# Second layer before the correction in PSUM, and score maxima subtracted by four full-array products

## The reference

```python
pos = grid_q[:, :, None, :] - grid_kv[:, None, :, :]
bias = jnp.sign(pos) * jnp.log1p(jnp.abs(pos))
bias = jax.nn.relu(bias @ cpb_w1 + cpb_b1)      # 2 -> 32
bias = jax.nn.relu(bias @ cpb_w2 + cpb_b2)      # 32 -> 32
bias = (bias @ cpb_w3 + cpb_b3)                 # 32 -> 1
sim = jnp.einsum('bhid,bhjd->bhij', qh, kh) + bias
attn = jax.nn.softmax(sim, axis=-1)
```

## Time and profile before

| | us |
|---|---|
| median of 3 runs | 929.76 (927.41 to 930.8) |
| the profiled execution | 930.51 |
| its span | 928.7 |
| TensorE matmuls busy | 848.8 (91%) |
| VectorE busy | 713.9 (77%) |
| ScalarE busy | 639.5 (69%) |
| GpSimd busy | 59.9 (6%) |
| granted TensorE clock, mean | 0.970 |

### The profile page before, as it was taken

One profiled execution on the slowest core, in us unless ns is written; L12 is line 12 of the kernel. 1 busy time (PEld: TensorE's weight loads), 2 busy tenths in 40 slices (PEclk: granted clock), 3 DMA queues, 4 the chain that ended last, 5 costly groups with the idle time before them and its releaser, 6 DMA issues.

```text
span 928.7 us, 34427 instructions
## 1 busy us (share of the span) xinstructions
PE 848.8 (91%) x15908; PEld 300.5 (32%) x15908; DVE 713.9 (77%) x472; ACT 639.5 (69%) x717; POOL 59.9 (6%) x40
## 2 busy tenths in 40 slices
PE   2179999989999999989999999999999999999936
PEld 1123323333333333323333333323333333333312
DVE  3678799898878659998878849989887749888411
ACT  1347768867777858877776857896777757777711
POOL 2200002120000002040000002040000000000000
PEclk9589999999999999999999999999999999999978
DMA  4210101011101101002011101002011101000010
GB/s 146 59 52 3 50 2 50 7 49 13 51 10 41 28 2 49 8 14 48 26 28 27 50 1 50 9 2 57 5 51 27 50 1 43 11 3 3 2 48 23
DMA packets 29535, 27.89 MB, mean 30 GB/s; under 512 B 22096, under 2 KB 24016, under 8 KB 29392
## 3 DMA queue, kind: packets, MB, share of 16 engines
q1 hardware_dynamic: 29392, 25.69, 10.6%
HBM read 23.05 MB, written 2.49 MB: 27 GB/s over the span
## 4 chain that ended last, share of the span: by engine, by line
PE 83%; DVE 8%; ACT 3%; DMA 3%; issue 2%; SPq 0%; POOL 0%; ACTq 0%; POOLq 0%; DVEq 0%
PE pair L771 29%; PE scores L783 24%; PE pair L766 9%; PE scores L795 3%; PE pair L914 3%; PE scores L880 3%; DVE h L565 3%; PE pair L924 3%; PE pair L873 2%; ACT h L426 2%; DVE big L668 2%; PE pair L891 1%; PE pair L905 1%; PE pair L818 1%; PE pair L854 1%
## 5 line engine op out<-in xcount | busy, mean ns | idle before, releaser
L426 ACT ACTIVATE h<-pair 128x1024 f32<-128x1024 f32 x512 | 496.5, 1022 | 201.9 <-PE pair L771 201.6
L565 DVE TENSOR_TENSOR h<-hx,hy 128x2048 f32<-128x2048 f32 x256 | 579.9, 2300 | 41.4 <-PE pair L771 41.1
L771 PE MATMUL pair<-h,wts 32*32 32x512 f32 x8192 | 346.6, 597 | 9.7 <-DVE h L565 9.7
L783 PE MATMUL scores<-h,wts 128*32 128x512 f32 x2048 | 273.6, 606 | 0.9 <-ACT h L426 0.9
L771 PEld LDWEIGHTS pair<-h,wts 32*32 32x32 f32 x8192 | 135.2, 103 | 29.3 <-DVE h L565 13.5
L766 PE MATMUL pair<-fy,u_rows 32*32 32x512 bf16 x4096 | 118.7, 386 | 27.4 <-DMA fy<-fy_dram 20.1
L783 PEld LDWEIGHTS scores<-h,wts 128*32 128x32 f32 x2048 | 43.6, 108 | 209.2 <-issue 208.4
L766 PEld LDWEIGHTS pair<-fy,u_rows 32*32 32x32 bf16 x4096 | 37.6, 88 | 196.7 <-issue 178.4
L691 DVE TENSOR_REDUCE neg_max<-pair 128x8 f32<-128x512 f32 x32 | 22.1, 691 | 70.3 <-PE pair L873 70.3
L306 POOL TENSOR_TENSOR conv_prod<-qpad,wts 128x288 f32<-128x288 f32 x16 | 21.6, 1379 | 440.3 <-ACT qpad L452 440.3
L406 POOL TENSOR_TENSOR big<-big,hat_x 128x512 f32<-128x512 f32 x16 | 35.5, 2248 | 119.0 <-DVE big L662 119.0
(11 more groups left out here) (87 smaller groups left out, 342.6 us busy)
## 6 DMA issues: line engine op xcount, KB each, us to landing
hx<-features_dram SPq DMA_DIRECT2D x64, 128.0 KB, 2.7
hy<-features_dram SPq DMA_DIRECT2D x64, 128.0 KB, 3.1
att_den<-reciprocals_dram SPq DMA_DIRECT2D x4, 512.0 KB
wts<-weights_dram SPq DMA_DIRECT2D x2, 960.0 KB, 8.5
fy_dram<-fy_part SPq DMA_DIRECT2D x96, 8.0 KB, 1.5
x<-x_dram SPq DMA_DIRECT2D x2, 512.0 KB, 5.9
fy<-fy_dram SPq DMA_DIRECT2D x64, 12.0 KB
out_dram<-x SPq DMA_DIRECT2D x2, 512.0 KB, 4.9
```

What stands on the lines that cost most here:

```text
L426: emptied("z", 2 * g + j, act.activation(h2[g % H2_BUFS][:, 2 * j:2 * (j + 1)].rearrange("p r n -> p (r n)"), pair_of("z", 2 * g + j)[:], ...
L565: dve.tensor_tensor(h1[g % H1_BUFS][:].rearrange("p c (y x) -> p c y x", x=W), hx[unit % 2][:, :, t].unsqueeze(2).broadcast_to([128, CT, H ...
L771: ins = pe.matmul(z[r][32 * c:32 * (c + 1)], w(l, "w2")[key[r], key[r]], h1[g % H1_BUFS][key[r], c], start=False, stop=True)
L783: ins = pe.matmul(scores[phase % 2][32 * r:32 * (r + 1)], w(l, "w3")[:, 32 * t:32 * (t + 1)], h2[g % H2_BUFS][:, r], start=False, stop=t = ...
```

## The change

Two edits and shifts of slots. (1) In `layer2` the 16 second-layer products come first, with `start=True` and the waits for the pairs, behind the wait for `h1_ready`; the 16 corrections follow with `start=False` and hand the pairs over, and the waits for `fy` and `u_rows` stand between them. (2) GpSimd copies `neg_max` to `neg_max_wide` (128 x 8 x 64, fp32r) in a new stage `widen_max`, which waits for the maxima and for the previous `max_off`; `score_max` waits for the copy of two phases before and not for `max_off`; `max_off` waits for the copy and takes four products of 128x128 in fp32r with an fp32r copy of the identity, which VectorE makes in its set-up. (3) `max_off` and `exp` move from step 2 to step 3 of the next phase; `exp_sums` from 3 to 4 and `attend` from 4 to 5; GpSimd's first hat products from 42 to 44, `sample` from 47 to 49, its copy to 51, keys and values to 52.

```diff
--- before.py
+++ after.py
@@ -80,20 +80,21 @@
     ("act", "features", 0): 36, ("act", "spread_out", 0): 37, ("dve", "features_sign", 0): 39,
     ("act", "distances", 0): 38, ("act", "distances", 1): 39, ("act", "distances", 2): 40,
     ("act", "distances", 3): 41, ("dve", "hats", 0): 42, ("dve", "hats", 1): 44,
-    ("pool", "hat_products", 0): 42, ("pool", "hat_products", 1): 44, ("dve", "hat_products", 0): 45,
-    ("dve", "hat_products", 1): 46, ("pe", "sample", 0): 47, ("dve", "sample_out", 0): 49,
-    ("pe", "keys_values", 0): 50, ("act", "keys_values_out", 0): 50,
+    ("pool", "hat_products", 0): 44, ("pool", "hat_products", 1): 44, ("dve", "hat_products", 0): 45,
+    ("dve", "hat_products", 1): 46, ("pe", "sample", 0): 49, ("dve", "sample_out", 0): 51,
+    ("pe", "keys_values", 0): 52, ("act", "keys_values_out", 0): 52,
 }
 
 AFTER_SLOTS = {
-    ("pe", "exp_sums", 0): 3, ("act", "exp_sums_out", 0): 3, ("pe", "attend", 0): 4,
-    ("act", "attend_out", 0): 4, ("dve", "reciprocal", 0): 8, ("dve", "divide", 0): 12, ("pe", "project", 0): 12,
+    ("pe", "exp_sums", 0): 4, ("act", "exp_sums_out", 0): 4, ("pe", "attend", 0): 5,
+    ("act", "attend_out", 0): 5, ("dve", "reciprocal", 0): 8, ("dve", "divide", 0): 12, ("pe", "project", 0): 12,
     ("dve", "residual1", 0): 14, ("pe", "mlp_up", 0): 14, ("act", "mlp_gelu", 0): 14, ("pe", "mlp_up", 1): 15,
     ("act", "mlp_gelu", 1): 15, ("pe", "mlp_up", 2): 19, ("act", "mlp_gelu", 2): 19, ("pe", "mlp_up", 3): 20,
     ("act", "mlp_gelu", 3): 20, ("pe", "mlp_down", 0): 22, ("dve", "residual2", 0): 24,
 }
 
-SOFTMAX_SLOTS = {("pe", "scores_t"): 1, ("dve", "score_max"): 3, ("pe", "max_off"): 2, ("act", "exp"): 2}
+SOFTMAX_SLOTS = {("pe", "scores_t"): 1, ("dve", "score_max"): 3, ("pool", "widen_max"): 3,
+                 ("pe", "max_off"): 3, ("act", "exp"): 3}
 TERMS_SLOT = 12
 
 PROLOGUE = {
@@ -223,6 +224,8 @@
         u_part = [sb(f"u_part{s}", [128, 128], BF16) for s in range(3)]
         u_rows = [sb(f"u_rows{l}", [128, 128], BF16) for l in range(LAYERS)]
         neg_max = [sb(f"neg_max{k}", [128, CHUNKS]) for k in range(2)]
+        neg_max_wide = sb("neg_max_wide", [128, CHUNKS, NKV], F32R)
+        ident_r = sb("ident_r", [128, 128], F32R)
         probs = sb("probs", [128, PAIRS, HW])
 
         pairs = [ps(f"pair{k}", HW) for k in range(RING)]
@@ -260,6 +263,7 @@
         h1_ready = sem("h1_ready")
         bias_added = sem("bias_added")
         scores_copied = sem("scores_copied")
+        max_widened = sem("max_widened")
         max_taken_off = sem("max_taken_off")
         exp_ready = sem("exp_ready")
         sums_packed = sem("sums_packed")
@@ -405,7 +409,16 @@
                 for k in (2 * part, 2 * part + 1):
                     pool.tensor_tensor(bilinear[:, k], hat_y[:, k], hat_x[:], ALU.mult).then_inc(bilinear_ready[0], 1)
 
-            stages = {"conv_products": conv_products, "hat_products": hat_products}
+            def widen_max(phase):
+
+
+                wait_emptied(pool, "scores_t", phase)
+                if phase:
+                    pool.wait_ge(max_taken_off, phase)
+                pool.tensor_copy(neg_max_wide[:], neg_max[phase % 2][:].unsqueeze(2).broadcast_to([128, CHUNKS, NKV]))\
+                    .then_inc(max_widened, 1)
+
+            stages = {"conv_products": conv_products, "hat_products": hat_products, "widen_max": widen_max}
             for p in range(2):
                 pool.memset(qpad[p][:], 0.0).then_inc(borders_zeroed, 1)
             for p in range(2):
@@ -687,7 +700,7 @@
             def score_max(phase):
                 wait_filled(dve, "scores_t", phase)
                 if phase >= 2:
-                    dve.wait_ge(max_taken_off, phase - 1)
+                    dve.wait_ge(max_widened, phase - 1)
                 emptied("scores_t", phase, dve.tensor_reduce(
                     neg_max[phase % 2][:], pair_of("scores_t", phase)[:, 0:HALF].rearrange("p (n j) -> p n j", j=NKV), AX_X,
                     ALU.max, negate=True))
@@ -735,6 +748,7 @@
             ordered(dve.memset(keys_t[0][:], 0.0))
             dve.memset(keys_t[1][:], 0.0).then_inc(setup_done, 1)
             dve.wait_ge(const_loaded, 16)
+            ordered(dve.tensor_copy(ident_r[:], cst("ident")))
             set_up(0)
             w1y_rows(0)
             for name, n in PLAN["dve"][-1]:
@@ -753,23 +767,23 @@
 
                 unit, h, t = g // UNIT_STEPS, g // STRIDES % 2, g % STRIDES
                 l = unit // PAIRS // B
+                z = [pair_of("z", 2 * g + r // 2)[:, bank(r % 2)] for r in range(ROWS)]
+                key = [slice(32 * r, 32 * (r + 1)) for r in range(ROWS)]
+                pe.wait_ge(h1_ready, g + 1)
+                for r in range(ROWS):
+                    if r % 2 == 0:
+                        turn("z", 2 * g + r // 2)
+                    for c in range(CT):
+                        pe.matmul(z[r][32 * c:32 * (c + 1)], w(l, "w2")[key[r], key[r]], h1[g % H1_BUFS][key[r], c],
+                                  start=True, stop=False)
                 if g % UNIT_STEPS == 0:
                     pe.wait_ge(fy_loaded[unit % 2], 16 * ROWS * (unit // 2 + 1))
                     pe.wait_ge(u_ready, l + 1)
-                z = [pair_of("z", 2 * g + r // 2)[:, bank(r % 2)] for r in range(ROWS)]
-                key = [slice(32 * r, 32 * (r + 1)) for r in range(ROWS)]
                 for r in range(ROWS):
-                    if r % 2 == 0:
-                        turn("z", 2 * g + r // 2)
                     y = fy[unit % 2][key[r], t, H // 2 * h:H // 2 * (h + 1)]
                     for c in range(CT):
-                        pe.matmul(z[r][32 * c:32 * (c + 1)], u_rows[l][key[r], 32 * c:32 * (c + 1)],
-                                  y.unsqueeze(2).broadcast_to([32, H // 2, W]), start=True, stop=False)
-                pe.wait_ge(h1_ready, g + 1)
-                for r in range(ROWS):
-                    for c in range(CT):
-                        ins = pe.matmul(z[r][32 * c:32 * (c + 1)], w(l, "w2")[key[r], key[r]], h1[g % H1_BUFS][key[r], c],
-                                        start=False, stop=True)
+                        ins = pe.matmul(z[r][32 * c:32 * (c + 1)], u_rows[l][key[r], 32 * c:32 * (c + 1)],
+                                        y.unsqueeze(2).broadcast_to([32, H // 2, W]), start=False, stop=True)
                     if r % 2:
                         filled("z", 2 * g + r // 2, ins)
 
@@ -874,12 +888,11 @@
                 filled("scores_t", phase, ins)
 
             def max_off(phase):
-                wait_emptied(pe, "scores_t", phase)
+                pe.wait_ge(max_widened, phase + 1)
                 for k in range(CHUNKS // 2):
-                    for n in range(2):
-                        ins = pe.matmul(scores[phase % 2][NKV * n:NKV * (n + 1), 128 * k:128 * (k + 1)],
-                                        neg_max[phase % 2][:, 2 * k + n:2 * k + n + 1].broadcast_to([128, NKV]),
-                                        cst("ident"), start=False, stop=True, skip_group_check=True)
+                    ins = pe.matmul(scores[phase % 2][:, 128 * k:128 * (k + 1)],
+                                    neg_max_wide[:, 2 * k:2 * (k + 1)].rearrange("p n j -> p (n j)"),
+                                    ident_r[:], start=False, stop=True, skip_group_check=True)
                 ins.then_inc(max_taken_off, 1)
 
             def over_keys(stage, seg, keys_to_channels):
```

## The result

The changed kernel took 940.13 us (median of 4 runs, 935.52 to 941.65) against 929.28 for the kernel before on the same chip (4 runs): 1.010 times as long, 95% interval 1.0079 to 1.0121. The forecast was 903, faster.

A forecast was written before the change was run, and what follows sets the result against it. TensorE's own sequence was taken as the bound: 1.42 us per phase over 24.9 phases gives 35, less 2 for dense stretches and 6 for small terms, 27 us: 930.5 to 903 us, range 886 to 926.

The forecast's parts named there:

- The step that failed: TensorE's open step: second layer first hides 0.19 of the correction's 0.23 us, front of step 1.31 instead of 1.50.
- The rule against it: TensorE weight loads: the skill says they overlap matmuls only on different row groups; by it the result is 912.
- Rival 1: TensorE's correction weights or second half come late, losing 0.1: step 2.41, 9 us less gained, 912 us; chance 0.16.
- ScalarE's loop: Ring pairs in open steps: pair free at 2.54 us, wanted at 2.37, so six steps per phase take 2.39.
- The maxima: TensorE's block taking maxima off the scores: 0.58 us with fp32r products instead of 1.03, 0.45 saved per phase.
- The dense stretches: Where VectorE prepares the next segment: 2 us charged (bounds 0 and 8) for copies beside it, no gain counted.
- The moved hat slots: GpSimd's hat products and sample move two later; copies at steps 35 and 43 lie around them.
- The copies by themselves: GpSimd's widening copies slow VectorE by 0.6 us each; VectorE at 85% in open stretches.
- The small terms: Exp, keys and values, unfilled waits, last phase and identity cast: together 6 us lost.

The follow-up runs named there:

- no_correction: The kernel before with the 16 correction products per step left out, so its output lacks the correction: 867.44 us, one run.
- after_aligned: The changed kernel, with GpSimd's convolution products behind the first segment held until step 31's first layer is done: 939.54 us, ratio 1.0099.
- max_dve: The kernel before plus 128x128 fp32r products for the maxima, widened by VectorE, slots and correction order as before: 926.24 us, ratio 0.995.

## Why the prediction was wrong

**The step that failed** is "the correction's 16 calls sit on the same 16 tiles and are released as these end, and stream 0.22. L783 can then start at 1.08 + 0.23 = 1.31". The first of them was released so, at 0.88; the second came 0.19 later and the others, 8 ns apart, behind it, and L797 (L783 before) started at 1.50: 0.19 late, and 0.19 is all that the edit was to save. The forecast had read the 0.19 by which L771 is longer behind a correction as something that L771 loses, and so as a thing that a clean array would save. It is the price of being the second group. The first half of the reading was right (the second layer alone takes 1.09 in no_correction). Putting the other group second moves it there: 0.23 + 1.27 before, 0.88 + 0.61 after, the same 1.50.

**The rule against it** was weighed on one row: nine weights loaded on busy row groups, so weights load ahead. Nine of 32 did before the first product started, and after the change two of 16. The Trainium skill (TensorE: Matmul & The Clock Gate, section What overlaps and what doesn't) says that they overlap only where the row group differs; the two loads at 240.63 speak against the rule's letter, the fourteen that waited for its effect. Whether any load ran ahead was the wrong question, since it did not keep the products from stopping: behind two early loads the second product stopped, and in the kernel before, behind nine, the ninth (at 403.32, its weights in by 403.14), both with their weights loaded. What stops them is not settled by these runs: not the format, the order of the groups or the order of the tiles.

**Rival 1** named this place ("the pattern is there today") and was priced at 0.1 a step where it is 0.19, which leaves nothing. (Its 0.35 less per phase is 0.32 by its own figures, and the phase's extras are 2.50 and not 2.48; neither changes a reading.) It was given 0.16, less than half of the forecast's chance; the row that spoke for it was the one the forecast rested on.

**ScalarE's loop** did not come to bind: at a step of 2.49 the pair, free some 2.56 after L777's start (241.72 and 1.02, from 240.18), is wanted at about 2.55. The forecast's 2.54 for it was right, and any step shorter than 2.49 would have met it.

**The maxima** were right: 0.58 forecast, 0.59 measured, 0.43 saved in most open phases. What the sum lacked is a term for the later slots of the maxima and the exp in the phases with the second half of the MLP: 0.7 to 0.9 us in each of three. Which wait there it is was not followed. **The dense stretches** were charged 2 us and cost 10.6. Two things were missing there. The moved hat slots were called harmless since "the copies at steps 35 and 43 lie around them"; the copy of step 43 stood on GpSimd's queue right in front of them, and with the later slot they ran into VectorE's. And the clock: TensorE fell to 1.2 GHz five times where it had fallen once. The copies by themselves were not dearer than thought: 11.3 us of VectorE's time for 32, 0.35 each where 0.6 was taken, and VectorE worked 115.5 of the 147 us from 204 on, 79% and not the forecast's 85. **The small terms** of 6 us held a clock that stays as it is; the first steps and the end cost 6.3 between them, much of it at the lower clock; the last section shows why little of that may belong to the change.

## What to carry to other kernels

When two groups of small products run back to back and the second is longer than it is alone, ask first whether the excess belongs to that group or to its place in the queue; a one-line run with the group left out and another with both groups made equal tell it before anything is reordered. Moving work to an idle GpSimd is only free where VectorE is not the pace-setter: check what stands behind the new instruction on its queue, and what VectorE's own operations take beside it. Before a loss is given to a wait, compare the granted clock of the same stretches: here it was 0.96, 0.98 and 0.96 in the stretches that had 0.98, 1.00 and 1.00 before. A gain on TensorE is collected only in the stretches where TensorE sets the pace, so count phases by stretch.

## What the runs showed of the hardware

A 128x512 copy on GpSimd takes 0.61 us alone and 2.61 when it starts beside a first layer of VectorE (2.28): it ends 0.47 behind that one. This agrees with the Trainium skill (SBUF — State Buffer, section SBUF: two separate sides): an exclusive lock, not a split of the bandwidth. But the convolution products of the kernel before, started within 0.05 us of each other, took 1.07 and 1.03 us each where VectorE's take 0.45 and GpSimd's 0.82 in the others, and why they ran so in one arrangement and one after another in the other is open. Products of 128x128 by 128 in fp32r ran as single records of 0.3 us, with 0.19 for a weight load, against two records per product in fp32. The clock of the first steps differed between kernels that do nearly the same there: the changed kernel was 2.95 us behind at step 3, after_aligned, whose edit touches nothing before step 28, 0.45. In max_dve, with the correction in front, the window from 56 to 66 us also has 0.83, and the kernel stood 2.1 us behind at step 3.

```profile
56.00:66.00 10.00, 8.88 (x164) 2.81 (x172) 10.00 (x5) 5.13 (x9) 0.00 (x0) 0.83 0.01 2
```

So differences of 2 to 3 us at the start, and as much at the end, belong to no part of the change that these runs could name.
